# A four-stage network on one core: Y accumulations paired around TensorE's side work, and the softplus moved ahead of the low part, in the state-space stage

## What is computed

```python
xi, z = split(xn @ W_in.T)                    # 128 + 128 channels, 1024 positions
xc = silu(causal_conv4(xi))                   # u
dt, Bm, Cm = split(xc @ W_x.T)                # 4 + 16 + 16
delta = softplus(dt @ W_dt.T + b_dt)
A = -exp(A_log)                               # 128 x 16
for t in range(1024):
    hst = hst * exp(delta[t] * A) + (delta[t] * xc[t]) * Bm[t]     # 16 states per channel
    y[t] = sum_n hst[n] * Cm[t, n]
y = (y + xc * Dp) * silu(z)
out = y @ W_out.T + x
```

## Time and profile before

| what | value |
|---|---|
| median of 3 runs | 3275.89 us (3267.01 to 3279.97) |
| the profiled execution | 3284.26 us, span 3282.4 us |
| PE busy | 2970.4 us (90%) |
| DVE busy | 2445.8 us (75%) |
| POOL busy | 2235.3 us (68%) |
| ACT busy | 2048.4 us (62%) |
| state-space stage, first scan to last | 2314.3 to 3269.0 us, 259 scans |
| the scan (L1776) | 593.2 us, 2290 ns each |
| product with C (L1784) | 316.2 us, 1221 ns each |

### The profile page before, as it was taken

How to read it: one execution, slowest core, us unless ns; L and a number is a source line. 1 busy time by engine, 2 the same in 40 slices (tenths; PEclk the granted TensorE clock), 3 DMA queues, 4 the chain that set the end, 5 groups by cost and what they waited for, 6 DMA issues and landing times. The chain is left out here.

```text
span 3282.4 us, 54459 instructions
## 1 busy us (share of the span) xinstructions
PE 2970.4 (90%) x17722; PEld 1138.4 (35%) x17722; DVE 2445.8 (75%) x2994; ACT 2048.4 (62%) x2269; POOL 2235.3 (68%) x904
## 2 busy tenths in 40 slices
PE   5999999999999999999998999875788888888887
PEld 2333343333333433334332333252233333333332
DVE  4888888888878888888871222233799999999998
ACT  3577777777767777777764333233556666666665
POOL 0488888888878888888874000001787887888878
PEclk7899999999989999999998999977899999999999
DMA  4477777777777777777775121013445355454444
GB/s 137 102 182 179 182 178 179 181 183 182 174 166 169 179 184 180 179 179 181 177 191 143 71 77 45 20 61 136 151 161 174 129 169 174 146 186 135 161 174 135
DMA packets 115106, 499.73 MB, mean 152 GB/s; under 512 B 19084, under 2 KB 19988, under 8 KB 82532
## 3 DMA queue, kind: packets, MB, share of 16 engines
q0 software_dynamic: 31824, 214.97, 31.1%
q1 hardware_dynamic: 83060, 281.86, 25.1%
HBM read 192.88 MB, written 39.65 MB: 71 GB/s over the span
## 5 line engine op out<-in xcount | busy, mean ns | idle before, releaser
L675 DVE TENSOR_REDUCE at_pmax<-at_ring 128x1 f32<-128x512 f32 x2048 | 1292.4, 684 | 269.1 <-PE at_ring L445 260.2
L634 ACT ACTIVATE at_probs<-at_sc 128x1024 f32<-128x1024 f32 x1024 | 992.6, 1021 | 381.3 <-PE at_sc L528 380.9
L738 POOL TENSOR_TENSOR at_prob_sums<-at_prob_sums,at_probs 128x2048 f32<-128x2048 f32 x189 | 926.3, 4901 | 7.7 <-ACT at_probs L634 7.5
L521 PE MATMUL at_sc<-at_QT,at_KT 32*128 32x512 f32 x4096 | 738.7, 638 | 6.2 <-issue 5.7
L1776 DVE TENSOR_TENSOR_SCAN ss_state<-ss_decay,ss_drive 128x1024 f32<-128x1024 f32 x259 | 593.2, 2290 | 66.7 <-ACT ss_decay L1713 34.0
L1807 POOL TENSOR_TENSOR ss_drive<-ss_du,ss_bsb 128x1024 f32<-128x1024 f32 x262 | 611.7, 2364 | 31.8 <-DVE ss_state L1776 27.8
L540 PE MATMUL at_O<-at_probs,at_V 128*32 128x512 f32 x4096 | 529.8, 606 | 1.6 <-issue 1.4
L1570 PE MATMUL ss_Y<-ss_seen,k_ident 128*128 128x512 f32 x1032 | 488.5, 595 | 0.0
L445 PE MATMUL at_ring<-at_KH,at_QH 32*128 32x512 bf16 x2048 | 456.8, 388 | 17.3 <-ACT at_KT L592 9.6
L1713 ACT ACTIVATE ss_decay<-ss_delta,k_a 128x1024 f32<-128x1024 f32 x260 | 290.6, 1118 | 253.6 <-DVE ss_state L1776 251.9
L738 POOL TENSOR_TENSOR at_prob_sums<-at_probs 128x2048 f32<-128x2048 f32 x63 | 303.4, 4816 | 73.5 <-ACT at_probs L634 73.5
(11 more groups left out here) (210 smaller groups left out, 2928.7 us busy)
## 6 DMA issues: line engine op xcount, KB each, us to landing
ss_bsb<-scratch_rows SPq DMA_DIRECT2D x265, 512.0 KB, 6.6
at_odd_sums<-at_probs POOLq DMA_DIRECT2D x126, 1024.0 KB, 7.7
at_odd_sums<-at_probs SPq DMA_DIRECT2D x63, 1024.0 KB, 5.1
at_prob_sums<-at_odd_sums POOLq DMA_DIRECT2D x63, 1024.0 KB, 7.6
scratch_attn<-at_att SPq DMA_DIRECT2D x64, 256.0 KB, 2.2
ss_xn<-scratch_xm SPq DMA_DIRECT2D x36, 256.0 KB, 5.1
at_xn<-scratch_xn SPq DMA_DIRECT2D x32, 256.0 KB, 6.3
k_att<-scratch_attn SPq DMA_DIRECT2D x16, 512.0 KB, 5.9
```

The lines of the kernel that those rows point to most:

```text
L521: nc.tensor.matmul(sc[:, h, :], KT[head(h), par, blk(kb)], QT[head(h), par, hs(half)], start=True, stop=False)
L634: nc.scalar.activation(probs[:, kb, two, :].rearrange("p h q -> p (h q)"), sc[:, two, :].rearrange("p h q -> p (h q)"), ACT.Exp, scale=SCA ...
L675: nc.vector.tensor_reduce(pmax[:, quad // 2, h, quad % 2:quad % 2 + 1], ring[:, unit[3], :], AX_X, ALU.max, negate=True).then_inc(max_done, 1)
L738: nc.gpsimd.tensor_tensor(prob_sums[:, half, :, :], before, probs[:, POOL_ADDS[n], :, :], ALU.add).then_inc(pool_sums, 1)
```

## The change

Five edits, all in the state-space stage.

1. PE's accumulation is left out at steps 4 and 11 and done twice at steps 5 and 12 (`LATE`): those of steps 3 and 4 at step 5, of steps 10 and 11 at step 12.
2. Z moves from step 12 to 13.
3. ACT: the table load and the logarithm come at step 11, `take_low` at 12, the load back at 13, the tanh and first copy of z at 14, the last at 15 (`plus_z`). POOL's gate moves from step 15 to step 1 of the next image.
4. First image: the logarithm comes right behind the exponential, ahead of the middle and low parts, and the first `decay` ahead of the load back and of z.
5. The clearing of `xn`, which the first load waits for, covers its six edge columns instead of all 1027.

```diff
--- before.py
+++ after.py
@@ -1405,7 +1405,8 @@
         LEAD = DEPTH - 1
 
         X0, X1, BC, DT, MID, LOW, Z = range(7)
-        UNIT_AT = {3: X0, 4: X1, 7: BC, 9: DT, 10: MID, 11: LOW, 12: Z}
+        UNIT_AT = {3: X0, 4: X1, 7: BC, 9: DT, 10: MID, 11: LOW, 13: Z}
+        LATE = (5, 12)
         UNITS = 6
 
         def loop_steps(b, par):
@@ -1428,7 +1429,7 @@
                 load(xn[0:C, KC - 1:], xn_d, b, xn_in)
                 load(xn[C:P, KC - 2:KC - 2 + S], xn_d, b, xn_in)
 
-            sp.wait_ge(cleared, 1)
+            sp.wait_ge(cleared, 3)
             load_x(0)
 
             def store(b):
@@ -1589,12 +1590,15 @@
             with pe.Fori(0, NB // 2) as j:
                 for g in range(2):
                     b = 2 * j + g
-                    before = (b, g, TURN - 1)
+                    older = before = (b, g, TURN - 1)
                     for now in loop_steps(b, g):
                         step(*now)
-                        add_state(*before)
+                        if now[2] in LATE:
+                            add_state(*older)
+                        if now[2] + 1 not in LATE:
+                            add_state(*before)
                         units(*now)
-                        before = now
+                        older, before = before, now
                         if now[2] == TURN - 1:
 
                             pe.wait_ge(yv_done, b + 2)
@@ -1625,6 +1629,8 @@
 
             def take_z(b, par):
                 nc.scalar.activation(gate[:, par, :], aux[:], ACT.Identity, scale=0.5).then_inc(z_done, 1)
+
+            def plus_z(b):
                 act.wait_ge(z_done, 3 * b + 1)
                 nc.scalar.activation(tanh_z[:], tanh_z[:], ACT.Identity, bias=1.0).then_inc(z_done, 1)
 
@@ -1660,9 +1666,9 @@
             def take_low(b, par):
                 act.wait_ge(aux_ready, UNITS * b + 5)
                 nc.scalar.activation(bc[4 * N:6 * N, par, :], aux[0:2 * N, :], ACT.Copy).then_inc(low_done, 1)
+
+            def soft_log(b):
                 nc.scalar.preload_act_table_set("natural_log_exp_and_others")
-
-            def soft_log(b):
                 act.wait_ge(abs_done, 2 * b + 2)
                 nc.scalar.activation(soft[1][:], soft[0][:], ACT.Ln, bias=1.0).then_inc(soft_done, 1)
 
@@ -1687,12 +1693,9 @@
             take_dt(0, 0)
             take_delta(0)
             soft_exp(0)
+            soft_log(0)
             take_mid(0, 0)
             take_low(0, 0)
-            soft_log(0)
-            back_to_exp()
-            bend_z(0)
-            take_z(0, 0)
             act.wait_ge(a_set, 1)
 
             def take_out(b):
@@ -1732,16 +1735,22 @@
                     soft_exp(b + 1)
                     take_mid(b + 1, 1 - par)
                 if n == 11:
+                    soft_log(b + 1)
+                if n == 12:
                     take_low(b + 1, 1 - par)
-                if n == 12:
-                    soft_log(b + 1)
                 if n == 13:
                     back_to_exp()
+                if n == 14:
                     bend_z(b + 1)
-                if n == 14:
                     take_z(b + 1, 1 - par)
+                if n == 15:
+                    plus_z(b + 1)
 
             make_decay(0, 0, 0)
+            back_to_exp()
+            bend_z(0)
+            take_z(0, 0)
+            plus_z(0)
             for n in range(TURN):
                 step(0, 0, n)
             with act.Fori(0, NB // 2) as j:
@@ -1752,7 +1761,9 @@
         @block.vector
         def _(dve):
 
-            nc.vector.memset(xn[:], 0.0).then_inc(cleared, 1)
+            nc.vector.memset(xn[0:C, 0:KC - 1], 0.0).then_inc(cleared, 1)
+            nc.vector.memset(xn[C:P, 0:KC - 2], 0.0).then_inc(cleared, 1)
+            nc.vector.memset(xn[C:P, KC - 2 + S:], 0.0).then_inc(cleared, 1)
             dve.wait_ge(later.ss, later.N_SS * DMA)
             dve.sem_inc(y_step, 1)
             dve.sem_inc(state_done, DEPTH)
@@ -1858,7 +1869,7 @@
                             add_xw(b, g)
                         if now[2] == 5:
                             make_u(b + 1, 1 - g)
-                        if now[2] == 15:
+                        if now[2] == 1:
                             make_gate(b + 1, 1 - g)
                         if now[2] == 12:
                             make_delta(b + 1, 1 - g)
```

## The result

| | before | after |
|---|---|---|
| median of 19 runs each | 3281.82 us (3267.01 to 3290.67) | 3261.27 us (3250.4 to 3271.67) |
| ratio, 95% interval | | 0.9949 [0.9939, 0.9958] |
| the profiled execution | 3284.26 us, span 3282.4 us | 3258.41 us, span 3256.4 us |
| DVE busy | 2445.8 us | 2442.9 us |
| PE busy | 2970.4 us | 2999.3 us |

The change makes the kernel 0.5% faster. By the ratio it saves 16.7 us of 3281.8, between 13.8 and 20.0; the two medians alone are 20.6 apart. The forecast was 3258 us, 18 less than the median then known, in a range of 3220 to 3282.

The account below looks back on a forecast made before the run. DVE was taken to pace the steps, with its idle waits the time to win. From the profiled 3284.3 us: - 52.0 for waits and start, + 34 for TensorE's falling clock, - 8.4 to the median's scale = 3258 us; range 3220 to 3282.

Parts of the forecast that it names:

- DVE's waits: Loop: DVE's waits of 0.40 us at step 6, 0.73 at 12 and 1.73 at 13 go, 45.6 us in all.
- The new wait at 13: DVE's product of step 13 waits 0.05 to 0.1 us for its spread; 0.8 us over 16 images.
- by a hair: ACT, steps 11 to 13: logarithm ends at 2714.72, `decay` of step 13 is due at 2714.77; the 1.73 us wait goes.
- The rival of the late logarithm: ACT's logarithm misses its time and up to 1.73 us an image returns: 3252 us, clock high; chance 0.04.
- POOL: Delta gets its input some 4 us earlier; `yv` waits about 3 us for Y, at no cost.
- First image: First scan at 2305.9 instead of 2314.31, third at 2314.9 instead of 2321.39; with the smaller clearing 7.2 us less.
- Sum without the clock: Waits removed 45.6 us, new waits 0.8, start 7.2 won: 52.0 us less, 3224 us on the median's scale.
- The clock: TensorE's clock falls in every image after narrow work from MID to LOW; 1.7 us lost per 3.4 us stretch.
- one stretch in three images of four, two in the fourth: Expected count of 3.4 us stretches at half clock per image; price 16 x 2.1 = 34 us.
- three low stretches: Rival: clock already down when LOW starts, three stretches in each image, 82 us lost against 52: 3305 us; chance 0.09.
- The held clock: Rival: TensorE's clock does not fall behind MID and LOW, nothing is taken back: 3224 us; chance 0.17.
- two stretches in nearly every image: Rival: LOW doubles at half clock; 16 x 3.4 = 54 us eats the 52: 3278 us, no change; chance 0.16.

Follow-up runs that it names:

- split kernel: The changed kernel with one half of an accumulation at step 11, the other half at step 12: 3225.63 us, ratio 0.9834; timed again 3222.14 us, 0.9837.
- the wide filler: The changed kernel plus one 128 x 128 x 512 matmul of zeros between the spread of step 11 and LOW: 3226.18 us, ratio 0.9842.
- the pair at 12 alone: The kernel before with only the accumulation left out at step 11 and done twice at step 12: 3301.5 us, ratio 1.0072.
- the narrow filler: The changed kernel plus one matmul of zeros with 32 rows, 32 columns and 512 positions ahead of LOW: 3281.0 us, ratio 0.998.
- the repeat: The changed kernel itself, unaltered, timed again beside other runs of the kernel before: 3266.82 us, ratio 0.9965.

## Why the prediction was right, point by point

**DVE's waits.** The waits for C at 12, for `decay` at 13 and at step 6 were to go, 45.6 us. They went: 46.2 by the scans' intervals, and the split kernel, where nothing takes their place, has them all. The new wait at 13 of 0.05 us with the clock up is 0.08 in the wide filler's images and nothing in the split kernel's.

**The logarithm "by a hair".** It was to end 0.05 us ahead of need. It ends at 2809.65, `decay` of step 13 runs from 2809.71 to 2810.83, and the scan that needs it starts at 2810.95: 0.12 us to spare, and no wait. Nor does a scan wait in the loop of the split kernel, where the clock leaves everything on time. The rival of the late logarithm is out, and with it the drain of about 1380 ns that the Trainium skill, "ScalarE: Activation LUTs", section "What ACT_TABLE_LOAD costs", adds to a load: the load at 2807.30 took 1.28 us and the logarithm started at 2808.59.

**POOL.** `yv` was to wait about 3 us for Y: 3.2 at most in 16 images, at no cost to DVE; no scan of the loop waits for a drive.

**First image.** Forecast 7.2 us less, of which 0.7 for the clearing: first scan at 2305.9 - 0.7 - 2264.74 = 40.5 us behind the start of the clearing and third at 49.5. Measured: 7.8 less, 40.13 and 48.87. The forecast's z did come between the first and second `decay`, and cost 1.65, where the forecast had 1.9.

**Sum without the clock.** 52.0 us forecast, 53.8 and 53.2 measured on the stage of the two split kernels, in which the clock holds and the work is otherwise the same.

**The clock.** The mechanism was right: the clock falls in every image of the change, and the pair at 12 alone (+24 us) and its removal (-1.5% instead of -0.5%) show that this pair is what brings it down. The rule named beside it (the Trainium skill, "TensorE: Matmul & The Clock Gate", section "HAM oscillation": the low clock comes when the array idles long between groups) does not give this result: by it the change would have taken 3224 us, and the narrow filler, which leaves PE busy 6.43 of 6.60 us, would have held the clock. The result of 3224 is real all the same, as the split and the wide filler show at 3222 to 3226 us, but in kernels that have wide matmuls between MID and LOW.

**The term that was mis-sized** is "one stretch in three images of four, two in the fourth", 16 x 2.1 = 34 us. Its price for each stretch was good (1.7 said; 1.6 on average in after, 1.69 in the wide filler). Its count was 20 and is 27, in both traces of the change. I reasoned that the two accumulations side by side bring the clock back, and it does rise while they run, in all 32 images of the two traces of the change; what I missed is when the fall comes. In 9 images it comes at LOW's end or just behind it (1.0 to 1.5 us after the scan of step 12 starts; LOW ends 1.3 after), as I had it, and one stretch is all. In 7 it comes 0.7 to 1.8 us before that scan starts, where LOW is about to run or has just begun (it starts 1.3 before); LOW then runs wholly or in part at half speed, and one or two further stretches are low. In both traces of the change the number follows the place: three stretches where the fall comes 1.0 to 1.8 us ahead of the scan, two where it comes 0.1 to 0.9 ahead, one where it comes behind. That is the rival "three low stretches", whose place I had right and which held in 4 images of 16, not in nearly all. The term is 42.3 us instead of 34.8 (with the 0.8 of the new waits), and on the trace the stage gains 11.9 where 18 were forecast.

The timed ratio says 16.7 us [13.8, 20.0], the repeat 11.5 [7.2, 15.7]; the two intervals overlap. The two profiled executions, 11.9 and 11.3, agree with the repeat. That the first executions had fewer low stretches is not borne out: their granted clock over the whole program is 0.9533 on average (19 runs), that of the repeat 0.9529 (11 runs), and one stretch more or less is about 0.0005 of it. So the nearness of 16.7 to the forecast 18 is in part luck: the term of the clock was 7.5 us too small, the sum without it 1 to 2 us too small, and the timed runs of the first set lay some 5 us above what the stage gains.

**The chances.** The held clock (3224), two stretches in nearly every image (3278) and three (3305) were each right for part of the images or for a neighbour kernel. That none held as a whole is why the sum lay between them.

## What to carry to other kernels

Before you move wide matmuls away from narrow ones to shorten a wait, look at what the granted clock does behind the narrow ones in the trace; here the move took away 0.73 us of waiting in an image and brought 2.6 us of new waiting. Half an accumulation of full width in that gap kept the clock up in all 16 images: not moving the accumulation, but splitting it, took all of the gain. And read a stage by its own first and last instruction: of the 26 us between the two spans, 14 came from stages that nobody had touched.

## What the runs showed of the hardware that was not expected

- **Low periods of three lengths.** Between the first scan and the last every low period took 3.4, 6.8 or 10.2 us, in all the traces that have one. The same code had each of the three in different images, in another order in the second execution. The fall drifts against the code: in after's images 8, 9 and 10 it comes 1.3, 1.3 and 1.5 us behind the start of scan 12, in images 4 and 12 it comes 1.8 and 1.7 us ahead of it.
- **A filler of 32 by 32 did not hold the clock, one of 128 by 128 mostly did.** In the profiled executions the stage took 1006.93 us with the first, 992.37 without a filler and 959.91 with the second, though both fillers add work.
- **Two lengths of a step.** A step of DVE without waits takes 3.47 us in some steps and 3.54 in others, in before and in after, by the time between the product's start and the next scan (1.15 or 1.22 us). It is why even images take 56.2 us and odd ones 56.4. Timeline of after, DVE:

```profile
2771.06 1.22 DVE L1795 TENSOR_TENSOR ss_seen<-ss_state,ss_C 128x1024 f32<-128x1024 f32 x1
2772.21 2.29 DVE L1787 TENSOR_TENSOR_SCAN ss_state<-ss_decay,ss_drive 128x1024 f32<-128x1024 f32 x1
...
2791.98 1.22 DVE L1795 TENSOR_TENSOR ss_seen<-ss_state,ss_C 128x1024 f32<-128x1024 f32 x1
2793.20 2.29 DVE L1787 TENSOR_TENSOR_SCAN ss_state<-ss_decay,ss_drive 128x1024 f32<-128x1024 f32 x1
```

  The short ones are steps 15 to 2, and in even images 3 to 5 too. In the trace the long ones have a wait instruction of DVE's sequencer (21 ns, the wait for `decay`) right ahead of the scan, behind the product; the short ones have none there. That goes with the lengths; no run changed it by itself.
